# Looped gathers, two row buffers, and a quarter of the weighing on GpSimd in a four-layer graph network

## What is computed

```
x = x + gnn(norm(x), edges) + mix(norm(x))
x = x + experts(norm(x))
```

```
layer 0, GAT, twice:  e = leaky_relu(a_s[src] + a_d[dst])      4 heads of 64
                      out = segment_sum(softmax_over_dst(e) * h[src], dst)
layer 1, sums:        out = segment_sum(h[src], dst)
layer 2, one head:    as GAT, with an edge term in e
layer 3, HGT, twice:  32 heads of 8; kw, m from src by edge type, q from dst
                      a = sum(kw * q);  ea = exp(a - segment_max(a))
                      out = segment_sum(m * ea, dst) / segment_sum(ea, dst)
```

## Time and profile before

| | us |
|---|---|
| median of 3 runs (10122.83 to 10169.24) | 10139.58 |
| the profiled execution | 10164.43 |
| its span | 10162.7 |

### The profile page before, as it was taken

The page is one execution under the profiler, slowest core; times in us unless marked ns, Lnnn a source line. Parts: engine busy times, 40 slices in busy tenths (PEclk is TensorE's granted clock), DMA queues, the critical chain, the costliest instruction groups (busy, mean ns, idle before and its releaser), DMA issues. The chain is left out here.

```text
span 10162.7 us, 113012 instructions
## 1 busy us (share of the span) xinstructions
PE 5216.2 (51%) x21780; PEld 3851.4 (38%) x21781; DVE 5407.4 (53%) x12276; ACT 1930.6 (19%) x4673; POOL 3755.9 (37%) x3506
## 2 busy tenths in 40 slices
PE   0554255445562745543824462907666676665523
PEld 0554133333342623332813342804444444443323
DVE  4764456656662243463155453144888558885723
ACT  0000134134310200011212210201333123330101
POOL 0288366256502346501135512221555025550023
PEclk9999877777775866775967675958888788887757
DMA  3122433133302723301723210923555136561025
GB/s 120 59 84 61 63 103 105 39 100 107 89 6 70 253 76 91 72 8 49 275 62 81 77 24 19 313 62 102 171 172 172 34 120 173 172 170 34 0 53 176
DMA packets 618474, 1020.90 MB, mean 100 GB/s; under 512 B 220197, under 2 KB 385674, under 8 KB 609578
## 3 DMA queue, kind: packets, MB, share of 16 engines
q0 software_dynamic: 197216, 489.93, 18.8%
q1 hardware_dynamic: 390539, 496.36, 15.1%
q10 hardware_dynamic: 30528, 32.52, 0.9%
HBM read 927.20 MB, written 90.46 MB: 100 GB/s over the span
## 5 line engine op out<-in xcount | busy, mean ns | idle before, releaser
L663 POOL DMA_INDIRECT l_hgt_ep_g<-l_hgt_tkm,keep_e_srct x832 | 905.9, 1089 | 1209.0 <-PE l_hgt_ep_out L738 622.3
L663 POOL DMA_INDIRECT l_gat_ep_g<-l_gat_th,keep_e_src x832 | 904.4, 1087 | 816.4 <-POOLq L92 365.4
L738 PE MATMUL l_hgt_ep_out<-l_hgt_ep_g,l_hgt_ep_here 128*126 128x288 f32 x1664 | 641.0, 546 | 563.9 <-issue 401.4
L738 PEld LDWEIGHTS l_hgt_ep_out<-l_hgt_ep_g,l_hgt_ep_here 128*126 128x126 f32 x1664 | 394.6, 248 | 736.0 <-issue 616.3
L738 PE MATMUL l_gat_ep_out<-l_gat_ep_g,l_gat_ep_here 128*126 128x264 f32 x1664 | 620.2, 530 | 75.4 <-issue 47.6
L465 POOL DMA_INDIRECT recs<-place_stage,place_pos x400 | 495.4, 1238 | 278.6 <-DVEq L454 157.0
L663 POOL DMA_INDIRECT l_ep_g<-l_table,keep_e_src x416 | 406.6, 977 | 403.4 <-PE l_ep_out L738 132.4
L1035 POOL DMA_INDIRECT l_sum_g<-l_table,keep_e_src x416 | 406.0, 976 | 272.8 <-issue 115.8
L886 DVE TENSOR_TENSOR l_hgt_edges_acc<-l_hgt_edges_acc,l_hgt_ep_stage 125x288 f32 x832 | 375.0, 451 | 236.4 <-ACT l_hgt_ep_stage L767 123.2
L738 PEld LDWEIGHTS l_gat_ep_out<-l_gat_ep_g,l_gat_ep_here 128*126 128x126 f32 x1664 | 407.5, 260 | 201.1 <-issue 84.4
L1046 PE MATMUL l_sum_out<-l_sum_g,l_sum_here 128*125 128x256 f32 x832 | 337.2, 547 | 277.1 <-DVE l_g L1071 138.8
(11 more groups left out here) (561 smaller groups left out, 12140.2 us busy)
## 6 DMA issues: line engine op xcount, KB each, us to landing
l_hgt_ep_hot<-locrow SPq DMA_DIRECT2D x208, 256.0 KB
f_moe_experts_w1b<-in_L_ffn_w SPq DMA_DIRECT2D x32, 1024.0 KB
f_moe_experts_w2b<-in_L_ffn_w SPq DMA_DIRECT2D x32, 1024.0 KB
f_moe_experts_w1b<-in_L_ffn_w SPq DMA_DIRECT2D x64, 512.0 KB
f_moe_experts_w2b<-in_L_ffn_w SPq DMA_DIRECT2D x64, 512.0 KB
f_moe_experts_w1b<-in_L_ffn_W SPq DMA_DIRECT2D x56, 512.0 KB
f_moe_experts_w2b<-in_L_ffn_W SPq DMA_DIRECT2D x56, 512.0 KB
l_gat_ep_hot<-locrow SPq DMA_DIRECT2D x104, 256.0 KB
```

Source lines behind the costliest of these rows:

```text
L663: gp.indirect_dma_start(g[:, k % 4, j, 0:W], None, table, bass.IndirectOffsetOnAxis(ap=idx[:, k * CT + j:k * CT + j + 1].bitcast(U32), axi ...
L738: pe.matmul(out[:, t % 4, 0:WO], here[:, b % 2, t, :], g[:, b, t, F:F + WO], start=True, stop=True).then_inc(s_out, 1)
```

## The change

GpSimd's gathers run in the loop of piped, 8 steps a turn, where they were in line. Since a gather in a loop takes its indices from a fixed place, each chunk's are first copied to ix, a ring of 8 places; the copy is one step ahead of the gather. stage has two buffers, by the chunk's parity: take of chunk k waits for keep and adds of chunk k-2; s_kept has four semaphores, by half and parity. For hgt VectorE weighs three tiles of four, and GpSimd the fourth (weigh_last, lag 4 in its list, behind the gather with lag 1); total waits for both.

```diff
@@ edge_pass
+        ix = ph.sb("ix", [128, 8, CT], I32)
-        stage = ph.sb("stage", [P + 1, CT, WO])
+        stage = ph.sb("stage", [P + 1, 2, CT, WO])
...
-            for k in range(NCH):
-                if k >= 4:
+            def indices(k, b):
+                gp.tensor_copy(ix[:, b, :], idx[:, bass.ds(k * CT, CT)]).then_inc(s_ix, 1)
+
+            def gather(k, b):
+                if later(k, 4):
                     gp.wait_ge(s_out, CT * (k - 3))
+                gp.wait_ge(s_ix, k + 1)
+                gp.nop(nofuse=True)
                 for j in range(CT):
-                    gp.indirect_dma_start(g[:, k % 4, j, 0:W], None, table,
-                                          bass.IndirectOffsetOnAxis(ap=idx[:, k * CT + j:k * CT + j + 1].bitcast(U32), axis=0)).then_inc(s_g[k % 4], 16)
+                    gp.indirect_dma_start(g[:, b % 4, j, 0:W], None, table,
+                                          bass.IndirectOffsetOnAxis(ap=ix[:, b, j:j + 1].bitcast(U32), axis=0)).then_inc(s_g[b % 4], 16)
+
+            def weigh_last(k, b):
+                gp.wait_ge(s_ex, k + 1)
+                gp.nop(nofuse=True)
+                m = g[:, b % 4, CT - 1, F:X].rearrange("p (h d) -> p h d", h=H)
+                gp.tensor_tensor(m, m, g[:, b % 4, CT - 1, X:X + H].unsqueeze(2).to_broadcast([128, H, D // H]), ALU.mult).then_inc(s_last, 1)
+            piped(gp, NCH, [(0, indices), (1, gather)] + ([(4, weigh_last)] if kind == "hgt" else []), 8)
...
@@ tensor, total
                         if kind != "ee":
                             pe.wait_ge(s_msg, QT * (k + 1))
+                        if kind == "hgt":
+                            pe.wait_ge(s_last, k + 1)
...
@@ scalar, take
-                    if later(k, 1):
-                        act.wait_ge(s_kept[h], 16 * k)
-                        act.wait_ge(s_added, CT * (k - 1) + HT * (h + 1))
+                    if later(k):
+                        act.wait_ge(s_kept[h + 2 * (b % 2)], every(k, b, 2, 16) - 16 if isinstance(k, int) else 8 * (k - b % 2))
+                        act.wait_ge(s_added, CT * (k - 2) + HT * (h + 1))
...
@@ vector, weigh
-                    m = g[:, b, 4 * q:4 * q + 4, F:X].rearrange("p g (h d) -> p g h d", h=H)
-                    v.tensor_tensor(m, m, g[:, b, 4 * q:4 * q + 4, X:X + H].unsqueeze(3).to_broadcast([128, 4, H, D // H]), ALU.mult).then_inc(s_msg, 1)
+                    n = 3 if kind == "hgt" else 4
+                    m = g[:, b, 4 * q:4 * q + n, F:X].rearrange("p g (h d) -> p g h d", h=H)
+                    v.tensor_tensor(m, m, g[:, b, 4 * q:4 * q + n, X:X + H].unsqueeze(3).to_broadcast([128, n, H, D // H]), ALU.mult).then_inc(s_msg, 1)
...
@@ edge_sums, gpsimd (indices and gather as above)
+            piped(gp, NG, [(0, indices), (1, gather)], 8)
```

More of the change, by code:

```diff
@@ L644, in edge_pass @@
             ex = ph.sb("ex", [128, 2, CT])
-        s_parts = ph.sem("parts")
+        s_ix, s_parts, s_last = ph.sem("ix"), ph.sem("parts"), ph.sem("last")
         s_g = [ph.sem(f"g{b}") for b in range(4)]
@@ L648, in edge_pass @@
         s_mask = [ph.sem(f"mask{b}") for b in range(2)]
-        s_kept = [ph.sem(f"kept{b}") for b in range(2)]
+        s_kept = [ph.sem(f"kept{b}") for b in range(4)]
         s_hot, s_found, s_prod, s_raw, s_rows, s_top, s_back, s_x, s_ex, s_msg, s_here, s_out, s_staged, s_added = (
@@ L683, in body @@
                     sp.wait_ge(s_staged, CT * k + HT * (h + 1))
-                    sp.dma_start(crow[bass.ds(k * CT + h * HT, HT), :].unsqueeze(0), stage[P:P + 1, h * HT:h * HT + HT, 0:D + H]).then_inc(s_kept[h], 16)
+                    sp.dma_start(crow[bass.ds(k * CT + h * HT, HT), :].unsqueeze(0), stage[P:P + 1, b % 2, h * HT:h * HT + HT, 0:D + H]).then_inc(s_kept[h + 2 * (b % 2)], 16)
                 return body
             piped(sp, NCH, ([(0, load_locs)] if kind != "ee" else []) + [(0, load_masks), (3, keep(0)), (3, keep(1))])
-            for h in range(2):
-                sp.wait_ge(s_kept[h], 16 * NCH)
+            for q in range(4):
+                sp.wait_ge(s_kept[q], 8 * NCH)
         @block.tensor
@@ L761, in body @@
                 def body(k, b):
[L762 to L764 removed]
+                    if later(k):
+                        act.wait_ge(s_kept[h + 2 * (b % 2)], every(k, b, 2, 16) - 16 if isinstance(k, int) else 8 * (k - b % 2))
+                        act.wait_ge(s_added, CT * (k - 2) + HT * (h + 1))
                     for t in range(h * HT, h * HT + HT):
                         act.wait_ge(s_out, CT * k + t + 1)
[L767 removed]
+                        act.copy(stage[:, b % 2, t, :], out[:, t % 4, 0:WO]).then_inc(s_staged, 1)
                 return body
@@ L885, in body @@
                     slot = acc[:, bass.ds(blks[t], 1), 0:WO].rearrange("p o c -> p (o c)")
-                    v.tensor_tensor(slot, slot, stage[0:P, t, :], ALU.add).then_inc(s_added, 1)
+                    v.tensor_tensor(slot, slot, stage[0:P, b % 2, t, :], ALU.add).then_inc(s_added, 1)
                 return (2 if t >= HT and kind != "hgt" else 1), body
@@ L1030, in _, with indices, gather @@
         def _(gp):
-            for i in range(NG):
-                if i >= 4:
+            def indices(i, b):
+                gp.tensor_copy(ix[:, b, :], idx[:, bass.ds(i * EG, EG)]).then_inc(s_ix, 1)
+            def gather(i, b):
+                if later(i, 4):
                     gp.wait_ge(s_out, EG * (i - 3))
+                gp.wait_ge(s_ix, i + 1)
+                gp.nop(nofuse=True)
                 for j in range(EG):
-                    gp.indirect_dma_start(g[:, i % 4, j, :], None, table,
-                                          bass.IndirectOffsetOnAxis(ap=idx[:, i * EG + j:i * EG + j + 1].bitcast(U32), axis=0)).then_inc(s_g[i % 4], 16)
+                    gp.indirect_dma_start(g[:, b % 4, j, :], None, table,
+                                          bass.IndirectOffsetOnAxis(ap=ix[:, b, j:j + 1].bitcast(U32), axis=0)).then_inc(s_g[b % 4], 16)
+            piped(gp, NG, [(0, indices), (1, gather)], 8)
         @block.tensor
```

2 lines of the change are left out of this document (added).

## The result

The changed kernel takes 10,824.12 us (median of 4 runs, 10,802.05 to 10,856.61), the kernel before 10,138.4 beside it: 1.067 times as long (95% interval 1.0641 to 1.0699), +686 us. The forecast was +290 us, 10,430, in a range from 10,190 to 10,700. Slower was right, and so was the place; the size was off by more than a factor of two. One run of a later experiment (E3) took 11,725.03 us at a granted clock of 0.68, the slower state of a chip; it counts in that experiment's median, and not in its ratio.

The account below looks back on a forecast made before the run. No engine was full; a TensorE-VectorE round of 8.39 us a chunk was taken to set the third layer's rate. Terms 310 - 40 + 20 = +290 us on 10,139.6 gave 10,430 us, range 10,190 to 10,700.

Parts of the forecast that it names:

- The closed round: Third layer: total, four gathers, GpSimd's multiply, next total; 9.94 us a chunk against 8.39, +310 us.
- Gather loops and index copies: GpSimd: added copies, no-ops, waits and loop turns cost 0 in GAT, layer-2 and third-layer passes, +20 us in the sums.
- Total: 3.07 us: Third-layer round: TensorE's total, first matmul to last, taken at 3.07 us a chunk from the profile before.
- third rival: Third layer: multiply waits behind VectorE's product and TensorE's clock falls; round 11.4 us, 10,720 us in all, chance 0.12.
- Quarter alone: Third layer: moving a quarter of the weighing to GpSimd makes the round 9.94 us, +310 us.
- the gap before the multiply: Third-layer round: 0.30 us on GpSimd between the last gather and the multiply, as before each gather.
- Row buffers: ScalarE's copies wait less: -15 us for each GAT pass, -10 for layer 2, 0 in the third layer; -40 us.
- Index copies in the sums: Layer-1 sums: slack is thin, so each of 104 chunks pays 0.2 us for its copy, +20 us.
- The other four passes: Two GAT passes, layer-1 sums and layer 2: -40 us from row buffers and +20 us from index copies.

Follow-up runs that it names:

- E3: The changed kernel with GpSimd's multiply moved ahead of the gathers in its list; 10,178.9 us, 1.0065 times the kernel before.
- E8: The changed kernel with GpSimd's multiply of each third-layer chunk done twice; 10,543.98 us, 1.0768 times the kernel before.
- E2: The kernel before with only GpSimd's weighing of one tile in four added, behind the gathers; 10,383.33 us, 1.0283 times the kernel before.
- E6: The changed kernel with GpSimd's steps of the edge passes written out instead of looped; 10,399.95 us, 1.0614 times the kernel before.
- E7: E6 with the index-copy wait and its no-op moved ahead of the wait for total; 10,091.49 us, 1.0316 times the kernel before.
- E10: E7 without GpSimd's multiply, VectorE weighing all four tiles, the sums also written out with that wait order; 9,998.36 us, 0.99 times the kernel before.
- E11: The changed kernel run again, unaltered, beside other runs; 10,730.01 us, 1.0614 times the kernel before.
- E12: The kernel before, unaltered, profiled again on another chip; third-layer passes of 850 and 857 us from first to last gather.
- E1: The changed kernel without GpSimd's multiply, VectorE weighing all four tiles; 10,070.71 us, 0.9964 times the kernel before.
- E15: E7 with a 128x512 GpSimd copy between the wait for total and the third-layer gathers; 10,693.98 us, 1.0551 times the kernel before.
- E14: E7 with nine unused 128x128 filler matmuls per third-layer chunk on TensorE; 10,288.38 us, 1.0167 times the kernel before.

## Why the prediction was right in direction and wrong in size

- **The closed round.** Right: total is released by GpSimd's multiply, the wait for crow is gone, and the loss is in the third layer. Changing the order takes it away (E3), doubling the multiply adds to it (E8). Of the 567 us in the third-layer windows this round, as forecast, has about half (E2).
- **The step that failed: "Gather loops and index copies ... In the third layer the copy lies in the wait for total: 0."** The copy does. The no-op does not: it holds the wait for total and so stands behind it, in the round I had just closed. Its price is 308 us (E6 against E7). With it out of the way the ratio was 1.0316 (E7), which on the first chip would be +320 us, against the +290 forecast. I asked what the new instructions cost GpSimd and not on which side of the wait each stands.
- **"Total: 3.07 us"** was the second error. It is TensorE's time in the round of before; with more idle time it gets the lower clock, 0.76 against 0.86, and takes 4.00 us. Of the no-op's 1.48 us a round some 0.53 is its own, 0.47 total's and 0.48 the gathers' (changed against E7). My third rival had the clock at +0.7 us and gave it 0.12; it was +0.93. Its other half, the multiply behind VectorE's product, didn't come: the multiply takes 0.64 us there, since the product has ended by then. That rival's 10,720 us came nearest to the measured time, and this is luck in part: it had the clock right, but 0.8 us of its round didn't come, and the no-op and the longer set, which it lacked, took that place.
- **Quarter alone.** +310 us forecast, +286 measured, with a round of 9.68 us against 9.94, but by errors that cancel in part: total +0.48, gathers -0.33, the gap before the multiply -0.28, the multiply -0.11. The gap of 0.30 us belongs to gathers, not to what follows them. The estimate of 0.55 us and a fixed part for the multiply, worked out from the 2.6 cycles an element of the Trainium skill (GPSIMD Engine Reference, § 3.1), fits the 0.64.
- **Row buffers.** -40 us forecast in the GAT and layer-2 passes, 0 in the third layer. Alone they give -89 and -99 us, 70 to 80 of it in the third layer: I priced the copy's wait at the 1.08 us of one add and wrote half of it off. Beside GpSimd's multiply they give nothing there, as forecast, since the round hides it: E2 with one row buffer and E7 with two have the same round, 9.68 and 9.67 us.
- **Index copies in the sums, +20 us.** Some 10 us were measured, and not for the reason given: with the copies, but written out and with the no-op ahead of the wait, the pass takes 594 us (E10), as before.
- **The other four passes** together were forecast at -20 us. In each pair of profiles from one chip the looped kernels are longer there: by 39 us in the first pair, 77 in E11 against E12, 48 and 92 in E1 and E3 against E2, whose four passes have the code of before. E10 is 8 us longer than E12. That speaks for the no-op or the loops here too, but isn't shown: the same code differs by up to 70 us from one chip to another (2,635 us in the first profile, 2,565 in E2).

## What to carry to other kernels

Before giving work to an idle engine, follow its queue from the new instruction back to what it waits for: if the consumer of the new result also releases something queued ahead of it, there is a closed round, and its length is the rate. Everything on the wait's far side counts in full then, a no-op included, and more than in full where a later start changes what runs beside it or lowers TensorE's clock. Put such work ahead of the wait in the list; and if both engines multiply from SBUF at the same moment, it gains nothing even there.

## What the runs showed of the hardware

- A no-op that holds a wait on GpSimd delays the indirect DMA behind it by 0.54 us (0.81 against 0.27); in the third layer a register loop costs nothing measurable (E6).
- A GpSimd instruction that starts while VectorE multiplies two operands from SBUF ends a fixed time behind that product in nearly all cases, however early it started: an indirect DMA 0.82 us behind it (E7, E15; away from it 0.94 to 1.28 us long), a 128x256 multiply 0.48 to 0.49 (E3; away from it 0.64).
- A delay of 0.22 us in the round made it 0.57 us longer, one of 0.54 us 1.4 us; near the clock's lower level, with total at 4.10 us, 0.61 us made it only 0.67 us longer (E8).
- Idle work for TensorE, 227 us of it in a pass, made that pass shorter, 944 us against 988 (E14, E7), through the granted clock.
- The kernel before took 9,792 us on one chip and 10,107 to 10,138 on others. The third-layer passes of E6 there were within 3 us of the changed kernel's elsewhere; the difference lies in the four other passes (606, 604, 544 and 555 us from first to last gather, against 682, 703, 604 and 656 in E11). The cause stays open.
